# Output and second feed-forward products with tokens on partitions, norms kept in rows, and another order of the tail

## The reference, cut to what matters

```python
for i in range(NUM_BLOCKS):                       # 4; D = 256, FF = 1024
    residual = x
    q = x @ Wq[i] + bq[i]; k = x @ Wk[i] + bk[i]; v = x @ Wv[i] + bv[i]
    Q = elu(q) + 1.0;  K = elu(k) + 1.0
    KV = einsum('nsh,nsh->nh', K, v);  Ksum = sum(K, axis=1)      # per sequence of 256 tokens
    V = Q * KV[:, None, :] / (Q * Ksum[:, None, :] + 1e-06)
    a = gelu(gelu(V @ Wo[i] + bo[i]))
    x = _ln(a + residual, ln1_s[i], ln1_b[i])
    residual = x
    h = gelu(x @ W1[i] + b1[i])
    f = gelu(h @ W2[i] + b2[i])
    x = _ln(f + residual, ln2_s[i], ln2_b[i])
```

## Time and profile before

| what | us |
|---|---|
| median of 3 runs (lowest, highest) | 1301.98 (1300.0, 1305.81) |
| the profiled execution | 1298.83 |
| its span, first to last instruction | 1297.0 |
| TensorE busy in it | 1125.7 (87%) |
| VectorE, ScalarE, GpSimd busy | 674.7, 602.0, 308.0 |

### The profile page before, as it was taken

The page is one execution under the profiler, slowest core; times in us unless marked ns, Lnnn a source line. Parts: engine busy times, 40 slices in busy tenths (PEclk is TensorE's granted clock), DMA queues, the critical chain, the costliest instruction groups (busy, mean ns, idle before and its releaser), DMA issues. The chain is left out here.

```text
span 1297.0 us, 15367 instructions
## 1 busy us (share of the span) xinstructions
PE 1125.7 (87%) x4442; PEld 622.0 (48%) x4442; DVE 674.7 (52%) x1912; ACT 602.0 (46%) x993; POOL 308.0 (24%) x317
## 2 busy tenths in 40 slices
PE   5639999999999999999999999766988768767872
PEld 4414444444444444444444445543555445456661
DVE  2256356545645663565467563555878855422221
ACT  3326535544554565455445533544665552024431
POOL 5120100100110011011020101224003674427775
PEclk9769999999999999999999999986998878889996
DMA  3210101130120121011350000258551216149997
GB/s 96 85 36 0 45 0 70 53 110 1 45 69 23 62 77 45 0 69 53 107 191 1 16 1 1 61 114 146 91 91 53 82 56 212 63 127 191 175 227 140
DMA packets 57431, 99.94 MB, mean 77 GB/s; under 512 B 10746, under 2 KB 38230, under 8 KB 57115
## 3 DMA queue, kind: packets, MB, share of 16 engines
q1 hardware_dynamic: 38219, 56.30, 16.4%
q0 software_dynamic: 19152, 42.92, 12.9%
HBM read 55.60 MB, written 53.00 MB: 84 GB/s over the span
## 5 line engine op out<-in xcount | busy, mean ns | idle before, releaser
L639 PE MATMUL b_ring<-left 128*128 128x512 f32 x480 | 210.9, 592 | 0.0
L639 PE MATMUL b_ring<-right,left 128*128 128x512 f32 x480 | 208.6, 592 | 0.0
L1144 POOL TENSOR_TENSOR b_rstd<-b_veps,b_mhalf 128x4 f32<-128x4 f32 x32 | 32.7, 1022 | 631.9 <-DVE b_veps L1210 631.9
L639 PE MATMUL b_ring<-XT,b_wqkv 128*128 128x512 f32 x384 | 175.0, 600 | 6.8 <-DMA b_wqkv<-in_wqkv 6.8
L639 PEld LDWEIGHTS b_ring<-left 128*128 128x128 f32 x480 | 90.3, 190 | 109.1 <-issue 109.1
L639 PEld LDWEIGHTS b_ring<-right,left 128*128 128x128 f32 x480 | 90.0, 190 | 108.3 <-issue 102.3
L913 ACT ACTIVATE left<-b_ring,b_cur 128x512 f32<-128x512 f32 x128 | 88.1, 688 | 74.8 <-PE b_ring L639 59.1
L639 PEld LDWEIGHTS b_ring<-XT,b_wqkv 128*128 128x128 f32 x384 | 71.5, 193 | 85.8 <-issue 78.6
L1315 DVE RECIPROCAL b_mixing<-b_mixing 128x1024 f32<-128x1024 f32 x16 | 104.8, 6553 | 0.5
L908 ACT ACTIVATE b_ffo<-b_ring,b_cur 128x512 f32<-128x512 f32 x32 | 22.0, 688 | 169.6 <-PE b_ring L639 157.7
L2065 ACT ACTIVATE a_ET<-a_pB 128x512 f32<-128x512 f32 x128 | 74.1, 595 | 43.4 <-PE a_pB L1815 42.3
(11 more groups left out here) (328 smaller groups left out, 1856.9 us busy)
## 6 DMA issues: line engine op xcount, KB each, us to landing
xe<-b_nil POOLq DMA_DIRECT2D x16, 1284.0 KB, 5.4
x_rows<-xe SPq DMA_DIRECT2D x32, 321.0 KB, 4.2
left<-in_w SPq DMA_DIRECT2D x8, 1024.0 KB, 5.3
x_wt<-in_wexp SPq DMA_DIRECT2D x16, 384.0 KB, 4.5
b_wqkv<-in_wqkv SPq DMA_DIRECT2D x4, 768.0 KB, 4.4
right<-qparts SPq DMA_DIRECT2D x16, 192.0 KB, 4.7
left<-qparts SPq DMA_DIRECT2D x16, 192.0 KB, 5.1
left<-in_wexp SPq DMA_DIRECT2D x6, 384.0 KB, 4.6
```

Of the source, the lines that this page charges most:

```text
L639: last = pe.matmul(bank[:, :], lhsT(k), rhs(k), start=(k == 0), stop=(k == n_k - 1))
L1144: pool.tensor_tensor(rstd[:, :], veps[:, :], mhalf[:, :], ALU.pow).then_inc(s_rs, 1)
```

## The change

- The products with wo and w2 are turned round: 128 tokens of the activation are stationary, 256 columns of the weights move (`rows_product`), two token tiles side by side in a bank. The result has tokens on partitions. A bank is then emptied by VectorE, which adds the bias from a row held on all partitions (`bias_added`); ScalarE's gelus run from SBUF to SBUF.
- s1, s2, `ffo`, `a1` and the residuals are in rows; the residual of the block input is kept in rows too (`xr`, in the space of `qn`). The turns of s1 and s2 into rows are gone. The norms apply gain (`gained`) and bias (`scaled`) on VectorE, with rows `rows1` and `rows2` that SyncE loads for each block. ScalarE's copies back are plain.
- The bias addition of the second w2 product stands on VectorE inside the next step's `first_norm`, and ScalarE's gelu of that half before the next step's first v.
- Bank waits are split: `s_free` for banks that ScalarE empties, `s_bi` for those that VectorE empties (`bank_free`).
- The tail has another order on every engine, four buffers for the transposed query rows in place of two, and the register load of `flag` stands ahead of the last maxima.

The diff, cut:

```diff
@@ SyncE
+            def load_rows(rows, first, b, loaded):
+                sp.dma_start(rows[:, :, :].rearrange("p i d -> p (i d)"),
+                             a["rows"][bass.ds(b, 1), first:first + 3, :].rearrange("b i d -> b (i d)").to_broadcast([P, 3 * D])).then_inc(loaded, 16)
...
                 if wait:
+                    sp.wait_ge(s_xn1, NC * b)
+                load_rows(rows1, 0, b, s_row1)
...
             with sp.Fori(1, BLOCKS) as b:
                 load(b, True)
+                sp.wait_ge(s_xn2, NC * b)
+                load_rows(rows2, 3, b, s_row2)
@@ TensorE
+                def rows_product(pair, n_k, src, weights, ready=None):
+                    bank = bank_free()
+                    for j in range(2):
+                        tile = slice((2 * pair + j) * P, (2 * pair + j + 1) * P)
+                        for k in range(n_k):
+                            if ready and j == 0:
+                                ready(k)
+                            last = pe.matmul(bank[:, j * D:(j + 1) * D], src[:, k, tile], weights[:, k, :],
+                                             start=(k == 0), stop=(k == n_k - 1))
+                    last.then_inc(s_full, 1)
...
                 qkv(0)
-                if ln1(s):
-                    pe.wait_ge(s_s1, NC * l + s)
-                    to_rows(s1, 2 * NC * l + n)
-                    n += 1
                 qkv(1)
...
-                if ln2(s):
-                    pe.wait_ge(s_s2, NC * l + s - 1)
-                    to_rows(s2, 2 * NC * l + n)
...
-                    w2_product(0, lambda k: pe.wait_ge(s_h, KF * (NC * l + s - 1) + k + 1))
+                    rows_product(0, KF, H, w2, lambda k: pe.wait_ge(s_h, KF * (NC * l + s - 1) + k + 1))
...
-                for m in range(KD):
-                    product(KD, lambda k: wo[:, k, m * P:(m + 1) * P], lambda k: mix[:, k, :])
+                for pair in range(KD):
+                    rows_product(pair, KD, mix, wo)
                 if ln1(s):
-                    w2_product(1)
+                    rows_product(1, KF, H, w2)
@@ ScalarE
-                    last = act.activation(X1T[:, m, c * CH:(c + 1) * CH], pR[m][:, :], ACT.Identity,
-                                          bias=col("ln1_b", m), scale=col("ln1_s", m))
+                    last = act.activation(X1T[:, m, :], pR[m][:, :], ACT.Copy)
...
+            def f_made(item, pair, added):
+                act.wait_ge(s_bi, added)
+                half = ffo[:, 2 * pair:2 * pair + 2, :]
+                act.activation(half, half, ACT.Gelu_apprx_tanh).then_inc(s_ff, 1)
...
                 for m in range(KD):
+                    if m == 0 and ln2(s):
+                        f_made(NC * l + s - 2, 1, adds)
...
+                act.wait_ge(s_bi, adds + KD + ln1(s))
+                act.activation(a1, a1, ACT.Gelu_apprx_tanh).then_inc(s_a, 1)
+                act.wait_ge(s_a, 2 * (NC * l + s) + 1)
+                act.activation(a1, a1, ACT.Gelu_apprx_tanh).then_inc(s_a, 1)
@@ VectorE
+            def scaled(dst, src, bias):
+                for j in range(TPC):
+                    last = dve.scalar_tensor_tensor(dst[:, j, :], src[:, j, :], rstd[:, j:j + 1], bias, ALU.mult, ALU.add)
+                return last
+
+            def bias_added(product, dst, pair, bias, bank):
+                dve.wait_ge(s_full, product + 1)
+                dve.tensor_tensor(dst[:, 2 * pair:2 * pair + 2, :], bank[:, :].rearrange("p (j d) -> p j d", j=2),
+                                  bias.unsqueeze(1).to_broadcast([P, 2, D]), ALU.add).then_inc(s_bi, 1)
+
+            def first_norm(s, l, link, n):
+                dve.wait_ge(s_s1, NC * l + s)
+                deviations(s1, link)
+                gained(s1, rows1[:, 1, :], link)
+                if ln2(s):
+                    last = products_before(s) - 1
+                    bias_added(last + NC * PER_STEP * l, ffo, 1, rows2[:, 0, :], ring[last % RING])
                 dve.wait_ge(s_rs, 2 * NC * l + n)
...
+                scaled(x1r[s % 2], s1, rows1[:, 2, :]).then_inc(s_xn1, 1)
```

More of the change, by code:

```diff
@@ L521, in columns_by @@
         def columns_by(s):
-            return sum((x % NC == 0 and x < ITEMS) + (ln1(x) and x % NC == 1) + (ln2(x) and x % NC == 2)
-                       for x in range(s + 1))
+            return sum((x % NC == 0 and x < ITEMS) + (ln1(x) and x % NC == 1) for x in range(s + 1))
         def norms_before(s):
@@ new lines, in late_w2 @@
+            def late_w2(pair):
+                bank = late_bank(END + KF + pair)
+                pe.wait_ge(s_free, A_END + KF - 1 + pair)
+                for j in range(2):
+                    tile = slice((2 * pair + j) * P, (2 * pair + j + 1) * P)
+                    for k in range(KF):
+                        if pair == 0 and j == 0:
+                            pe.wait_ge(s_h, KF * (ITEMS - 1) + k + 1)
+                        last = pe.matmul(bank[:, j * D:(j + 1) * D], H[:, k, tile], w2[:, k, :], start=(k == 0), stop=(k == KF - 1))
+                last.then_inc(s_full, 1)
@@ L821, in _ @@
                 late_w1(f)
[L822 removed]
+            down(0)
             for f in range(KF // 2, KF):
```

348 lines of the change are left out of this document (170 added, 178 removed).

## The result

| what | before | after |
|---|---|---|
| median (lowest, highest), us | 1301.53 (1300.0, 1305.81), 4 executions | 1268.88 (1263.46, 1274.91), 4 executions |
| ratio, with its 95% interval | | 0.9744 (0.9693 to 0.9794) |
| the profiled execution, its span | 1298.83, 1297.0 | 1263.46, 1261.8 |

The change takes 2.6% off. The forecast was 1268.6 us in a range of 1262 to 1281. The page of the changed kernel, in the order of the earlier trace rows: busy time, share and instructions first, then tenths in 40 slices, now 31.5 us each.

What follows compares the result with a forecast made beforehand. In the steps only TensorE's own work counts, in the tail order and waits. -26.0 + 0.4 + 0.2 - 5 - 2 - 1 = -33.4 us gives 1265.4 profiled, 1268.6 us as a median, range 1262 to 1281.

Steps and rivals of the forecast that it cites:

- Part 1: Full steps: the transposes of s1 and s2 into rows go, 1.74 us a step, and a wait of 0.24 us.
- Part 2: w2 and wo products with 256 columns per matmul: 0.2163 us a record, 0.12 us more per step.
- Part 3: Steps: VectorE gets 5.5 us more, 30 of about 43; results come in time, the second norm's margin 2.2 us.
- the columns of x1: Steps: ScalarE's two copies are done 0.4 us before TensorE is ready for them, the smallest margin.
- chain of step 1: Step 1, without a second w2 product as cover: needs 9.95 us, a wait of 1.35, step ends 0.4 us later.
- Tail a: From the end of step 15 to the end of the last w2 product: 43.1 us, +0.2 us.
- Tail b: From the last w2 product to the first head maxima: operands land and are handed over at 36 us, -5 us.
- Tail c: From the first maxima to their transposes: 23.0 us becomes 21.0 as the new order spreads VectorE's waits, -2 us.
- end of the phase: From the last transposes to the next phase: register load goes ahead of the last maxima, -1 us, between 0 and -3.
- 1: Rival: the tail gives nothing, operands and maxima wait or the clock falls as now; 1275.4 us, chance 0.12.
- 3: Rival: slower, the added weight loads stand on TensorE's path; up to +70 us, 1338 us, chance 0.03.
- 2: Rival: VectorE becomes late for the output product beyond 2.2 us of margin; one us over gives 1282.6 us, chance 0.09.

Runs made afterwards that it cites:

- experiment 7: Changed kernel with ScalarE copying the first columns ahead of the half gelu in the tail; 1263.77 us, ratio 0.9699.
- after: The changed kernel itself, against the kernel before; median 1268.88 us, ratio 0.9744, profiled execution 1263.46 us.
- second series: The changed kernel run again unchanged, as control; median 1268.24 us, ratio 0.9716, profiled execution 1267.73 us.
- experiment 1: The changed kernel run again with nothing changed, to see its spread; median 1268.24 us, ratio 0.9716.
- experiment 2: Changed kernel with the old tail order, two query buffers and late register load put back; 1274.41 us, and 1282.6 us when run again.
- experiment 3: Kernel before with w1 products in matmuls of 256 or 128 columns in place of 512; 1299.4 us and 1308.21 us.

## Why the prediction was right, point by point

- **What bounds the kernel.** In the steps only TensorE's own time counted: shown from both sides. 1.75 us of TensorE's work put back cost 1.75 a step, 1.2 us of VectorE's cost nothing. In the tail it was otherwise, as the prediction said: order and waits.
- **Part 1, transposes and the wait behind them.** Forecast -1.98 us a step, measured with the shapes -1.885 to the forecast's -1.86 (26.39 over 14). No wait came back at those transposes in the full steps.
- **Part 2, the shapes.** Forecast 0.2163 us for a record of 256 columns, measured 0.2159 (32 records from 341.78 to 348.69). The row in the tail was the right witness.
- **Part 3, VectorE's margins.** 30.13 us of work forecast as 30; 2.46 us of margin forecast as 2.2. The smallest margin, the columns of x1, was forecast as 0.4 and is 0.44 (ScalarE's copies end at 326.73, the w1 products start at 327.17); no run tests it. The chain of step 1 took 9.72 in place of 9.95; the prediction's own terms without the late bias add up to 9.8, so 0.15 of that is a slip. By its way of counting the wait there was 1.1 and not 1.35 (the row names 0.98), and step 1 was 0.07 longer, not 0.4.
- **What the prediction missed: step 0.** It costed the row loads for the next block's w1 alone and said that they cost nothing. It didn't follow the queue to the last operand that GpSimd's additions onto h wait for, nor ask what runs beside those additions. The missing term was +1.95 us. The trace of before had its sign in it, a tensor_scalar of 3.37 us in step 0 against 1.23 in the earlier trace rows.
- **Tail a, the term that was mis-sized.** Forecast +0.2, measured +1.8, and up to +4.7 in other traces of the same code. The reason was named (a half gelu that waits for VectorE ahead of the copy that TensorE wants); the wait grew from 1.17 to 2.43. But it was laid out with the durations of full clock, and 1.7 of the 1.8 us are the clock that fell behind that wait (experiment 7): with the clock up tail a would be 43.0, the forecast's 43.1.
- **Tail b.** Forecast by the landing of the operands at 36, measured 36.01. The third part is stored 19.53 us behind the last w2 product (forecast 19.7), and the last operand issued 10.84 later (10.8). But the landing is only just the limit. In `after` TensorE waited 0.29 us for it; in five of the nine traces with this order it had not finished its own work in front by then, and the maxima still started at 35.6 to 37.1. That TensorE's own list would be as long as the way of the operands the prediction didn't work out, so the hit at 36.01 is in part chance. -6.25 against -5: the value taken lay between the 6 and the 4 that it had laid out.
- **Tail c and the end of the phase.** -2.9 and -1.4 against -2 and -1, and in the nine traces with the new order tail c took 18.2 to 20.3 us.
- **The median.** Predicted through the distance of the profiled execution to the median, 3.15 us. After the change that distance is 5.4 and in the second series 0.5: the sum of the parts was -33.1 against a forecast of -33.4, and the rest, 2.1 us in the later phases, is the spread shown in experiment 1. That the median came within 0.3 us of the forecast is partly luck, twice over. The sum of the parts was right because misses met: +1.95 in step 0 and +1.6 in tail a against -1.25, -0.9 and -0.4 in the rest of the tail and -0.7 in the steps. The forecast of the blocks alone, -25.6 against -26.3, doesn't rest on that.
- **The range.** Its lower end, 1262, allows 4 us more in the tail, but the bound of -9 for the whole tail leaves 2.2 beyond the -6.8 forecast for it; by the bounds the end would be 1264. The measured median lies inside either way.
- **The rivals.** 1 falls by the tail's 8.8 us in the table and by experiment 2, 3 by experiment 3. 2 is a true mechanism whose threshold the kernel stays 2.46 us ahead of.

## What to carry to other kernels

Where one engine is busy without a gap, count its instructions and let the rest be margins: the sum then holds (here to 0.03 us a step), and each margin is a threshold that one idle instruction can test. A transfer moved ahead in a queue is paid by whoever waits for the last one behind it, so follow that queue to its end in the prologue too, and look at what runs beside the work that now starts later. A wait of 2.4 us on TensorE can cost more by the clock behind it than by itself; it is worth looking for an instruction, on the engine that TensorE waits for, that needn't stand first.

## What the runs showed of the hardware

- Fresh weights of 128 rows for every 256 columns cost 2.5 ns a load, for every 128 columns 5.8 ns (0.2158 and 0.1116 us a record). The second is neither fully hidden nor a load that stands on TensorE's path.
- A tensor_scalar of 2048 elements went from 1.23 to 3.3 us, and a three-operand instruction of 256 elements from 0.42 to 2.44, with GpSimd's tensor_tensor beside them.
- TensorE's granted clock fell to the level of 1.2 GHz behind the tail's first wait where that was 2.43 us or more, in nine traces of nine, and stayed at 2.4 GHz where it was 1.17 or 1.18, in five of five. How long it stays low differs between executions of one kernel (tail a 46.1 and 47.6 us in the two with the old order); in two traces of the changed kernel the same code of the later phases took 411.0 and 417.6 us.
